# A graph layer over 98 groups of 512 edges: the edge attributes of the next group in five transfers of two tiles, each behind another product of the present group

## The chip, the cores and the metric

The kernel runs on one core of one Trainium2 chip. The metric is device microseconds of one execution; of three runs of the kernel before, the median is 1954.64 us (1952.21 to 1956.52). The profile is of one further execution of the same program, by the hardware profiler.

## The reference

A graph layer over 50,000 nodes of 160 values (64 scalars and 32 vectors of 3) and 50,000 edges of 32 attributes (8 scalars, 8 vectors):

```python
tp = fctp_messages(node_features[col], edge_attr_tensor, W1, W2, W3, W4)
messages = tp @ Wm + bm
agg = jax.ops.segment_sum(messages, row, num_segments=N_NODES)
upd = jnp.concatenate([node_features, agg], axis=-1) @ Wu + bu
# node_features + upd is returned; around it:
x = _layernorm(x + _L0_gnn_ref(...), axis=-1)
```

`fctp_messages` multiplies every node value of an edge's source node with every edge attribute and contracts the products with W1 to W4. Everything is float32.

## The kernel before

The edges are cut into 98 groups of 512 (`GE`), the columns of a tile. For each group the kernel

- gathers the 512 node rows by index with four indirect DMAs of 128 rows, issued by POOL (`gather`, L310, into `xg`). Their landing lets ACT spread the vector part (`spread_x`, L366), and PE transpose it into PSUM (L618, L626);
- holds the edge attributes as ten tiles of 512 columns in `e_sb`, in which the 32 attributes are repeated over the 128 partitions. There are two such buffers, for even and odd groups. SP loads them from DRAM (`load_e`, L213 and L217): 2.62 MB a group, the repetition included;
- multiplies the transposed nodes with the edge tiles on DVE into `prod`: `times_xs` (L490, tiles 0 to 3), three times `times_xv` (L502: tiles 0, 1 and 4, 5; then 0, 1 and 6, 7; then 0, 1 and 8, 9) and `times_y` (L510, tiles 4 to 9). These are six counts of the semaphore `multiplied` (`USES` is 6; `times_y` gives two). L518 adds two products;
- contracts the products on PE (L638, L645), forms the messages (L691, L692), sums the rows of edges with the same target within a pair of tiles (L702 to L705), and copies the sums out on ACT (L420, `summed`);
- adds them to the table `agg` in DRAM with four indirect DMAs of 128 rows that accumulate (`scatter`, L327), issued by POOL. As two rows of the same node must not be added at once, the scatters go in pairs, and a pair waits until the pair before has landed (semaphore `scattered`).

There is no scheduler: each engine runs a program written out by hand, in slots, one for each group. In slot s DVE multiplies group s. POOL issues, in this order, two gathers of group s+2, a pair of scatters of group s-3, the other two gathers, the other pair. PE transposes s+1 and contracts s-1. SP, in `slot`, loads the indices of s+4 and of s+1 (`load_dst`, `load_src`; the second waits until DVE has computed the row indices of group s-3, L527 and L536, which comes right after `times_xs` of slot s; it includes `row_sb`, 256 KB), and then, by `load_e`, the edge attributes of s+2. During slots 0 to 3 SP also writes the start value of `agg` (50 transfers of 640 KB, L236); the first scatter waits for all of them. After the last group a second part of 49 steps reads `agg` and the nodes, adds, normalizes and writes the result (L563 to L588, L447, L347); its node loads (L275) start when PE is done with the groups, its first load of `agg` (L281) when the last scatter has landed.

An engine's instructions wait in the order in which they stand. Semaphores alone tie the engines together.

Of the kernel before, what the change touches and what calls it, by code (L numbers as in the profile page):

```python
# [20 lines left out]
GE = P * TILES  # L21
D = 160
NS, NV, DE = 64, 32, 32
ET = 10
NPROD = 22
USES = 6
# [7 lines left out]
def shift(group, by, m=M1):  # L34

    j, u = group
    return j + (u + by) // m, (u + by) % m


def number(group, m=M1):  # L40
    return group[0] * m + group[1]


def at_least(group, least, m=M1):

    return not isinstance(group[0], int) or number(group, m) >= least
# [14 lines left out]
def build(nc, x, x_rows, x_t, dst_idx, src_idx, src_row, e_rep, w1, w2, w3, w4, wm_t, wu, bu, ident, eye4,  # L61
# [11 lines left out]
    with ExitStack() as ctx:  # L73
# [9 lines left out]
        def sem(name):  # L83
            return ctx.enter_context(nc.semaphore(name))
# [22 lines left out]
        e_sb = two("e_sb", [P, ET, GE])  # L107
# [48 lines left out]
        es_in = [sem(f"es_in{u}") for u in range(M1)]  # L156
        ev_in = [sem(f"ev_in{u}") for u in range(M1)]
# [7 lines left out]
        sp_passed = sem("sp_passed")  # L165
# [23 lines left out]
        multiplied = sem("multiplied")  # L189
# [12 lines left out]
        def hold(engine, passed):  # L202
            engine.sem_inc(passed, 1)
# [2 lines left out]

        @block.sync
        def _(sp):
            def load_e(g):
                if at_least(g, 2):  # L210

                    sp.wait_ge(multiplied, number(g) * USES - 2 * USES + 4)
                sp.dma_start(e_sb[g[1] % 2][:, 0:4, :], e_rep[number(g), :, 0:4, :].unsqueeze(0).to_broadcast([32, 4, 4, GE])  # L213
                             ).then_inc(es_in[g[1]], 16)
                if at_least(g, 2):
                    sp.wait_ge(multiplied, number(g) * USES - 2 * USES + 6)
                sp.dma_start(e_sb[g[1] % 2][:, 4:ET, :], e_rep[number(g), :, 4:ET, :].unsqueeze(0).to_broadcast([32, 4, ET - 4, GE])  # L217
                             ).then_inc(ev_in[g[1]], 16)

            def load_dst(g):  # L220
                if at_least(g, 4):
# [17 lines left out]
            def slot(s):  # L239
                live = lambda d: not isinstance(s[0], int) or 0 <= number(s) + d < n_groups  # L240
                if live(4):
                    load_dst(shift(s, 4))
                if live(1):
                    load_src(shift(s, 1))
                if live(2):
                    load_e(shift(s, 2))
                if isinstance(s[0], int) and number(s) < 4:
                    for k in range(PIECES * (number(s) + 2) // 6, PIECES * (number(s) + 3) // 6):
                        start_table(k)

            for b in range(4):
                load_dst((0, b))
            load_e((0, 0))
            sp.dma_start(start_rows[:, :].rearrange("p (r d) -> p r d", r=SET_ROWS),
                         bu.unsqueeze(0).to_broadcast([P, SET_ROWS, D])).then_inc(start_rows_in, 16)
            for to, frm in (
# [6 lines left out]
            ):  # L263
                sp.dma_start(to, frm).then_inc(consts_in, 16)  # L264
            load_src((0, 0))
            load_e((0, 1))
            sp.wait_ge(start_rows_in, 16)
            for k in range(PIECES * 2 // 6):
                start_table(k)
# [196 lines left out]
        def _(dve):  # L466
# [16 lines left out]

            def times_xs(g):
                dve.wait_ge(A_copied, number(g) + 1)
                dve.wait_ge(es_in[g[1]], g[0] * 16 + 16)
                if at_least(g, 2):

                    dve.wait_ge(rounds, number(g) * ROUNDS - 2 * ROUNDS + 4)
                nc.vector.tensor_tensor(prod[g[1] % 2][:, 0:4, :],  # L490
                                        ps[:, t_bank(g, 0), :].unsqueeze(1).to_broadcast([P, 4, GE]),
                                        e_sb[g[1] % 2][:, 0:4, :], ALU.mult).then_inc(multiplied, 1)

            def times_xv(g, i):
                dve.wait_ge(t_ready, number(g) * USES + 2 + i)
                if i == 0:
                    dve.wait_ge(ev_in[g[1]], g[0] * 16 + 16)
                    if at_least(g, 2):
                        dve.wait_ge(rounds, number(g) * ROUNDS - ROUNDS)
                edge = e_sb[g[1] % 2][:, 0:6 + 2 * i, :] if i == 0 else e_sb[g[1] % 2][:, 0:ET, :]  # L500
# [336 lines left out]
```

## Time and profile before

| | |
|---|---|
| median of three runs | 1954.64 us |
| the profiled execution: its time / its span | 1957.06 us / 1954.9 us |
| PE busy | 1664.8 us (85%) |
| DVE busy | 1548.7 us (79%) |
| POOL busy | 1082.8 us (55%) |
| ACT busy | 894.1 us (46%) |
| bytes moved by DMA | 491.06 MB, mean 251 GB/s |
| share of the 16 DMA engines: SP's queue / POOL's queue | 51.2% / 27.2% |

Busy is the time in which an engine executes an instruction. The issue of a DMA counts as busy on POOL, since POOL writes its own transfers, and doesn't on SP. A DMA's transfer itself is seen in the share of the DMA engines and in the moment at which a waiting instruction is released. In rows of the timeline the bracket at the end is how long the engine was idle before the instruction, and what ended that.

### The profile page before, as it was taken

How to read it: one execution, taken by the hardware profiler on the slowest of the kernel's cores; microseconds unless marked ns; L12 is line 12 of the kernel's file. 1: busy time of each engine (PE TensorE's matmuls, PEld its weight loads, DVE VectorE, ACT ScalarE, POOL GpSimd, SP SyncE). 2: the span in 40 equal slices, each digit the busy share in tenths (PEclk: the TensorE clock that was granted, in tenths of full speed). 3: DMA queues.
4: the chain of work that ended last, by engine and by line, in shares of the span. 5: the costliest groups of instructions: out<-in, count | busy, mean ns of one | idle time of the engine just before them, and what ended most of it. 6: DMA issues, size and time to landing. Idle time of an engine off the chain costs nothing.

```text
span 1954.9 us, 35058 instructions
## 1 busy us (share of the span) xinstructions
PE 1664.8 (85%) x11964; PEld 896.5 (46%) x11964; DVE 1548.7 (79%) x1726; ACT 894.1 (46%) x1721; POOL 1082.8 (55%) x837
## 2 busy tenths in 40 slices
PE   2744999999999999999999999999999999478883
PEld 1312444445444444444444454444444444356662
DVE  2553888888888888888888888888888887089994
ACT  1302444444444444444444444444444444268885
POOL 2104667666666666666666666766666666311110
PEclk9876999999999999999999999999999999889996
DMA  7997777777777777777777777777777875789994
GB/s 246 380 361 234 237 233 224 235 237 231 228 228 226 226 227 226 233 237 236 222 235 240 237 232 229 228 227 225 228 232 238 237 235 121 235 331 420 418 413 178
DMA packets 177240, 491.06 MB, mean 251 GB/s; under 512 B 49560, under 2 KB 101848, under 8 KB 152108
## 3 DMA queue, kind: packets, MB, share of 16 engines
q1 hardware_dynamic: 94892, 381.38, 51.2%
q0 software_dynamic: 82304, 109.12, 27.2%
q8 instruction: 24, 0.39, 0.1%
q14 instruction: 20, 0.16, 0.0%
HBM read 393.52 MB, written 96.88 MB: 251 GB/s over the span
## 4 chain that ended last, share of the span: by engine, by line
DMA 41%; issue 21%; POOL 21%; PE 6%; DVE 5%; SPq 2%; ACT 2%; POOLq 1%; ACTq 0%; DVEq 0%
DMA agg<-summed,row_idx 29%; POOL agg L327 15%; POOL xg L310 6%; DMA prod<-agg 5%; DMA agg<-start_rows 5%; DMA xg<-in_x_rows,dst_sb 3%; DVE stats L582 2%; DVE prod L563 2%; PE ps L638 1%; PE ps L645 1%; SPq L264 1%; DVE mv L588 1%; ACT spread L366 1%; DMA e_sb<-in_e_rep 1%; PE ps L691 1%
## 5 line engine op out<-in xcount | busy, mean ns | idle before, releaser
L327 POOL DMA_INDIRECT agg<-summed,row_idx x392 | 645.0, 1645 | 469.5 <-DMA agg<-summed,row_idx 311.2
L502 DVE TENSOR_TENSOR prod<-ps,e_sb 128x2048 f32<-128x2048 f32 x294 | 663.7, 2285 | 144.1 <-PE ps L645 136.7
L645 PE MATMUL ps<-prod,w_sb 128*32 128x512 f32 x3136 | 753.9, 603 | 0.8 <-ACT S_sb L378 0.8
L310 POOL DMA_INDIRECT xg<-in_x_rows,dst_sb x392 | 411.4, 1050 | 187.8 <-issue 121.8
L366 ACT ACTIVATE spread<-xg 128x1536 f32<-128x1536 f32 x98 | 145.5, 1485 | 435.6 <-DMA xg<-in_x_rows,dst_sb 426.5
L510 DVE TENSOR_TENSOR prod<-ps,e_sb 128x3072 f32<-128x3072 f32 x98 | 328.1, 3348 | 0.0
L490 DVE TENSOR_TENSOR prod<-ps,e_sb 128x2048 f32<-128x2048 f32 x98 | 224.0, 2285 | 111.2 <-ACT A_sb L372 84.1
L645 PEld LDWEIGHTS ps<-prod,w_sb 128*32 128x32 f32 x3136 | 148.6, 109 | 156.4 <-issue 156.4
L638 PE MATMUL ps<-prod,w_sb 128*32 128x512 f32 x1176 | 207.6, 605 | 0.0
L626 PEld LDWEIGHTS ps<-ident_sb,spread 128*128 128x128 f32 x1176 | 127.6, 143 | 170.3 <-issue 121.6
L638 PE MATMUL ps<-prod,sum_sb 128*32 128x512 f32 x1176 | 187.9, 598 | 0.0
L447 ACT ACTIVATE prod<-prod,shift_n,rstd 128x160 f32<-128x160 f32 (+1 forms) x392 | 166.6, 507 | 42.3 <-DVE shift_n L575 42.3
L378 ACT ACTIVATE S_sb<-ps 128x512 f32<-128x512 f32 x98 | 58.8, 600 | 277.4 <-PE ps L645 277.4
L691 PE MATMUL ps<-wc_s,S_sb 128*128 128x160 f32 x784 | 180.8, 311 | 1.2 <-ACT S_sb L378 1.2
L626 PE MATMUL ps<-ident_sb,spread 128*128 128x128 f32 x1176 | 174.0, 285 | 6.7 <-DVE prod L502 4.5
L692 PE MATMUL ps<-wc_v,V_sb 97*128 97x160 f32 x784 | 170.8, 298 | 0.0
L396 ACT ACTIVATE apart<-row_sb,neg_src 128x256 f32<-128x256 int32 x392 | 166.3, 500 | 0.0
L691 PEld LDWEIGHTS ps<-wc_s,S_sb 128*128 128x128 f32 x784 | 124.7, 189 | 83.4 <-issue 81.3
L420 ACT ACTIVATE summed<-ps 128x644 f32<-128x644 f32 x98 | 69.3, 707 | 182.7 <-PE ps L705 135.2
L702 PE MATMUL ps<-msg,same 128*128 128x161 f32 x392 | 100.0, 337 | 45.9 <-ACT msg L412 45.6
L347 POOL DMA_DIRECT2D out<-prod x49 | 26.2, 535 | 203.3 <-ACT prod L447 199.2
L634 PE MATMUL ps<-A_sb,w_sb 64*128 64x512 f32 x392 | 114.4, 661 | 27.3 <-DVE prod L502 27.3
(63 smaller groups left out, 1826.6 us busy)
## 6 DMA issues: line engine op xcount, KB each, us to landing
e_sb<-in_e_rep SPq DMA_DIRECT2D x98, 1536.0 KB
e_sb<-in_e_rep SPq DMA_DIRECT2D x98, 1024.0 KB
agg<-start_rows SPq DMA_DIRECT2D x50, 640.0 KB, 5.4
prod<-agg SPq DMA_DIRECT2D x48, 640.0 KB, 10.4
out<-prod POOLq DMA_DIRECT2D x48, 640.0 KB, 7.7
row_sb<-in_src_row SPq DMA_DIRECT2D x98, 256.0 KB
prod<-in_x_t SPq DMA_DIRECT2D x25, 640.0 KB, 11.9
e_sb<-in_x_t SPq DMA_DIRECT2D x24, 640.0 KB, 12.9
```

The lines of the kernel that those rows point to most:

```text
L310: nc.gpsimd.indirect_dma_start(xg[g[1] % 2][:, q, :], None, x_rows, bass.IndirectOffsetOnAxis(dst_sb[g[1]][:, q:q + 1].bitcast(U32), 0)).t ...
L327: nc.gpsimd.indirect_dma_start(agg, bass.IndirectOffsetOnAxis(row_idx[g[1]][:, q:q + 1].bitcast(U32), 0), summed[g[1]][:, q // 2, q % 2 * ...
L396: last = nc.scalar.activation(apart[:, q, :], pair, ACT.Abs, bias=neg_src[g[1] % 2][:, q:q + 1])
L447: last = nc.scalar.activation(y[0:parts, cols], y[0:parts, cols], ACT.Identity, bias=shift_n[v][0:parts, q:q + 1], scale=rstd[v][0:parts, ...
L490: nc.vector.tensor_tensor(prod[g[1] % 2][:, 0:4, :], ps[:, t_bank(g, 0), :].unsqueeze(1).to_broadcast([P, 4, GE]), e_sb[g[1] % 2][:, 0:4, ...
L502: nc.vector.tensor_tensor(prod[g[1] % 2][:, 4 + 4 * i:8 + 4 * i, :].rearrange("p (a b) e -> p a b e", b=2), ps[:, t_bank(g, 1 + i), :].uns ...
L510: nc.vector.tensor_tensor(prod[g[1] % 2][:, 16:22, :].rearrange("p (f i) e -> p f i e", f=2), ps[:, first:first + 2, :].unsqueeze(2).to_br ...
L626: last = nc.tensor.transpose(ps[:, t_bank(g, 1 + i), q * P:(q + 1) * P], spread[:, q, i * P:(i + 1) * P], ident_sb[:, :])
L638: return nc.tensor.matmul(ps[32 * i:32 * i + 32, V_BANK, :], w, prod[g[1] % 2][:, tile, :], start=start, stop=stop)
L645: return nc.tensor.matmul(ps[32 * quarter:32 * quarter + 32, S_BANK, :], w[:, 32 * half:32 * half + 32], prod[g[1] % 2][:, tile, :], start ...
L691: nc.tensor.matmul(to, S_sb[g[1] % 2][:, q * P:(q + 1) * P], wc_s[:, :], start=True, stop=False)
L692: last = nc.tensor.matmul(to, V_sb[g[1] % 2][:, q * P:(q + 1) * P], wc_v[:, :], start=False, stop=True)
```

## The change

Instead of two transfers (tiles 0 to 3, then 4 to 9) the attributes of a group now come in five of two tiles each, in the order 2, 0, 4, 6, 8. Transfer `step` of group g is issued when `multiplied` has reached (g-1) x 6 + step: the first once all of group g-2 is multiplied, the others one by one behind the products of group g-1. In slot s SP now loads group s+1, not s+2; slot 0 loads none, as groups 0 and 1 are loaded ahead without waits. A small semaphore instruction (`hold`) stands between each wait and its transfer. DVE waits for 32 counts instead of 16 before `times_xs` and for 48 before the first `times_xv`.

```diff
-            def load_e(g):
-                if at_least(g, 2):
-
-                    sp.wait_ge(multiplied, number(g) * USES - 2 * USES + 4)
-                sp.dma_start(e_sb[g[1] % 2][:, 0:4, :], e_rep[number(g), :, 0:4, :].unsqueeze(0).to_broadcast([32, 4, 4, GE])
-                             ).then_inc(es_in[g[1]], 16)
-                if at_least(g, 2):
-                    sp.wait_ge(multiplied, number(g) * USES - 2 * USES + 6)
-                sp.dma_start(e_sb[g[1] % 2][:, 4:ET, :], e_rep[number(g), :, 4:ET, :].unsqueeze(0).to_broadcast([32, 4, ET - 4, GE])
-                             ).then_inc(ev_in[g[1]], 16)
+            def load_tiles(g, t):
+                return sp.dma_start(e_sb[g[1] % 2][:, t:t + 2, :],
+                                    e_rep[number(g), :, t:t + 2, :].unsqueeze(0).to_broadcast([32, 4, 2, GE]))
+
+            def load_e(g, spaced=True):
+
+
+                for step, t in enumerate((2, 0, 4, 6, 8)):
+                    if spaced:
+                        sp.wait_ge(multiplied, (number(g) - 1) * USES + step)
+                        hold(sp, sp_passed)
+                    load_tiles(g, t).then_inc(es_in[g[1]] if t < 4 else ev_in[g[1]], 16)
...
-                if live(2):
-                    load_e(shift(s, 2))
+                if live(1) and at_least(s, 1):
+                    load_e(shift(s, 1))
...
-            load_e((0, 0))
+            load_e((0, 0), spaced=False)
...
-            load_e((0, 1))
+            load_e((0, 1), spaced=False)
...
-                dve.wait_ge(es_in[g[1]], g[0] * 16 + 16)
+                dve.wait_ge(es_in[g[1]], g[0] * 32 + 32)
...
-                    dve.wait_ge(ev_in[g[1]], g[0] * 16 + 16)
+                    dve.wait_ge(ev_in[g[1]], g[0] * 48 + 48)
```

The other engines' instructions stay in their order. On SP, in a slot of the steady part, there stands before (`dst_sb`, `src_sb`, `row_sb` are the indices, `e_sb` the attributes; this is slot 6):

```order
103 L223 DMA dst_sb<-in_dst_idx 128x4 [waits x_gathered2]
104 L230 DMA src_sb<-in_src_idx 128x4 [waits idx_step,apart_done]
105 L231 DMA row_sb<-in_src_row 128x512
106 L213 DMA e_sb<-in_e_rep 128x1x2048 [waits multiplied]
107 L217 DMA e_sb<-in_e_rep 128x1x3072 [waits multiplied]
```

and now (slot 8, the first of the loop's body), where ISA rows are the semaphore instructions and REGISTER_ALU rows compute the loop's waits:

```order
107 L231 REGISTER_ALU [waits idx_step]
108 L232 ISA [waits apart_done]
109 L232 DMA src_sb<-in_src_idx 128x4
110 L233 DMA row_sb<-in_src_row 128x512
111 L218 REGISTER_ALU
112 L210 ISA [waits multiplied]
113 L210 DMA e_sb<-in_e_rep 128x1x1024
114 L218 REGISTER_ALU
115 L210 REGISTER_ALU [waits multiplied]
116 L210 DMA e_sb<-in_e_rep 128x1x1024
117 L218 REGISTER_ALU
118 L210 ISA [waits multiplied]
```

The two transfers of 2048 and 3072 columns have become five of 1024 (the last three stand below the rows shown), each with its own wait.

During the start, SP before issues the attributes of group 2 in slot 0, between the 16th and the 17th transfer of the start value:

```order
40 L230 DMA src_sb<-in_src_idx 128x4
41 L231 DMA row_sb<-in_src_row 128x512
42 L213 DMA e_sb<-in_e_rep 128x1x2048 [waits multiplied]
43 L217 DMA e_sb<-in_e_rep 128x1x3072 [waits multiplied]
44 L236 DMA agg<-start_rows 128x1280 [waits table_set1]
```

and now none there, and those of group 2 a slot (nine transfers of the start value) later:

```order
38 L232 DMA src_sb<-in_src_idx 128x4
39 L233 DMA row_sb<-in_src_row 128x512
40 L238 DMA agg<-start_rows 128x1280 [waits table_set1]
...
48 L238 DMA agg<-start_rows 128x1280 [waits table_set0]
49 L225 DMA dst_sb<-in_dst_idx 128x4 [waits x_gathered1]
50 L232 DMA src_sb<-in_src_idx 128x4
51 L233 DMA row_sb<-in_src_row 128x512
52 L210 DMA e_sb<-in_e_rep 128x1x1024 [waits multiplied] x5
```

Between the first and the last transfer of the start value there stood four groups of attributes (2 to 5), and there stand three now (2 to 4).

## Rows read from the trace of the kernel before

**Rows 1.** Windows view: stretch, its us, busy of the engines, PEclk, DMA share, GB/s.

```profile
300.00:1600.00 1300.00, 1226.76 (x8677) 622.10 (x8676) 1124.67 (x656) 597.05 (x1066) 881.91 (x654) 1.00 0.77 231
```

**Rows 2.** Timeline of DVE: start us, us, instruction, and the idle time before it.

```profile
176.26 2.29 DVE L490 TENSOR_TENSOR prod<-ps,e_sb 128x2048 f32<-128x2048 f32 x1 [39.10 <-ACT A_sb L372]
...
816.02 2.28 DVE L490 TENSOR_TENSOR prod<-ps,e_sb 128x2048 f32<-128x2048 f32 x1
819.83 4.49 DVE L502 TENSOR_TENSOR prod<-ps,e_sb 128x2048 f32<-128x2048 f32 x2 [1.11 <-PE ps L645]
...
827.70 3.35 DVE L510 TENSOR_TENSOR prod<-ps,e_sb 128x3072 f32<-128x3072 f32 x1
832.32 2.29 DVE L490 TENSOR_TENSOR prod<-ps,e_sb 128x2048 f32<-128x2048 f32 x1 [1.27 <-ACT A_sb L372]
...
848.50 2.28 DVE L490 TENSOR_TENSOR prod<-ps,e_sb 128x2048 f32<-128x2048 f32 x1
...
863.32 2.28 DVE L490 TENSOR_TENSOR prod<-ps,e_sb 128x2048 f32<-128x2048 f32 x1
...
1642.49 2.29 DVE L490 TENSOR_TENSOR prod<-ps,e_sb 128x2048 f32<-128x2048 f32 x1 [1.28 <-ACT A_sb L372]
```

**Rows 3.** Waits of PE, 300 to 1600 us: us in total, times, longest.

```profile
PE ps L618 <- DMA xg<-in_x_rows,dst_sb: 34.9, 30, 1.2
```

**Rows 4.** Groups of POOL's instructions, 300 to 1600 us: busy us, mean ns, idle before.

```profile
L327 POOL DMA_INDIRECT agg<-summed,row_idx x328 | 539.9, 1646 | 319.1 <-DMA agg<-summed,row_idx 243.6 <-issue 70.7 <-ACT spread L366 3.7
L310 POOL DMA_INDIRECT xg<-in_x_rows,dst_sb x326 | 342.9, 1052 | 99.3 <-issue 99.3
```

**Rows 5.** Waits of POOL, 300 to 1600 us.

```profile
POOL agg L327 <- DMA agg<-summed,row_idx: 243.6, 91, 4.4
```

**Rows 6.** Timeline of POOL, between 812 and 889 us.

```profile
812.43 1.58 POOL L327 DMA_INDIRECT agg<-summed,row_idx  x1 [0.30 <-ACT spread L366]
...
819.85 1.61 POOL L327 DMA_INDIRECT agg<-summed,row_idx  x1 [3.23 <-DMA agg<-summed,row_idx]
...
882.52 1.61 POOL L327 DMA_INDIRECT agg<-summed,row_idx  x1 [2.19 <-DMA agg<-summed,row_idx]
...
888.94 1.61 POOL L327 DMA_INDIRECT agg<-summed,row_idx  x1 [0.30 <-issue]
```

**Rows 7.** Timeline of SP's queue, the loads issued between 813 and 820 us.

```profile
813.01 0.57 SPq L213 DMA_DIRECT2D e_sb<-in_e_rep  x1
816.27 0.54 SPq L217 DMA_DIRECT2D e_sb<-in_e_rep  x1
...
819.46 0.38 SPq L231 DMA_DIRECT2D row_sb<-in_src_row  x1
```

**Rows 8.** Windows view (columns as in rows 1), four stretches.

```profile
814.00:817.30 3.30, 3.30 (x30) 2.30 (x31) 3.30 (x2) 1.36 (x4) 2.01 (x3) 1.00 0.91 303
...
818.50:822.50 4.00, 4.00 (x30) 1.38 (x25) 2.83 (x3) 2.67 (x6) 2.35 (x2) 1.00 1.01 407
...
826.00:829.00 3.00, 1.82 (x18) 0.71 (x20) 3.00 (x2) 0.72 (x1) 2.39 (x3) 1.00 0.22 40
...
63.00:157.00 94.00, 44.48 (x272) 20.48 (x266) 41.51 (x23) 17.39 (x32) 5.67 (x6) 0.76 0.96 370
```

**Rows 9.** Timeline of POOL: the first scatter, and two of the last.

```profile
162.53 1.62 POOL L327 DMA_INDIRECT agg<-summed,row_idx  x1 [65.95 <-issue]
...
1661.15 1.54 POOL L327 DMA_INDIRECT agg<-summed,row_idx  x1 [2.55 <-DMA agg<-summed,row_idx]
...
1684.27 1.54 POOL L327 DMA_INDIRECT agg<-summed,row_idx  x1 [7.72 <-DMA agg<-summed,row_idx]
```

**Rows 10.** Timeline of SP's queue behind the last group.

```profile
1673.72 4.11 SPq L275 DMA_DIRECT2D prod<-in_x_t  x8
...
1715.98 1.28 SPq L281 DMA_DIRECT2D prod<-agg  x3
```

**Rows 11.** Timeline of DVE behind the last group.

```profile
1681.23 0.22 DVE L527 SCALAR_TENSOR_TENSOR moved<-summed,dup_sb,trash_sb 128x4 f32<-128x4 f32 x1 [9.91 <-ACT summed L420]
```

## The prediction

> **What bounds the kernel now.** I begin with the steady part, 300 to 1600 us, which holds 82 of the 98 groups (82 `times_xs` stand there, a quarter of 328 scatters, [rows 4]). 1300 us / 82 = 15.85 us a group. PE is busy 1226.8 of 1300 us and DVE 1124.7 [rows 1]: PE looks like the bound. The timeline of DVE says otherwise. The starts of `times_xs` lie 16.30, 16.18 and 14.82 us apart [rows 2]. So when nothing is late PE and DVE do a group in 14.82 us, and the mean is 1.03 us above that.
>
> The view of waits names what is late: PE waits for the gathered nodes 30 times in this stretch [rows 3]. Each time two long groups follow each other, as 816.02 to 848.50 does: 32.48 us instead of 2 x 14.82, or 2.84 us lost. 30 x 2.84 = 85 us, which is all of the 1300 - 82 x 14.82 = 85 us above the floor.
>
> Gathers are late because POOL issues them, between scatters. The issue itself takes, per group, 4 x 1.646 + 4 x 1.052 us and eight gaps of 0.30: 6.58 + 4.21 + 2.40 = 13.19 us [rows 4, 6]. That is under 14.82. The rest of 15.85, 2.66 us, is waiting: POOL waits for the landing of scatters 91 times for 243.6 us [rows 5]; without the 0.30 that stand there anyway, 216.3 us, or 2.64 a group and 2.38 a wait. POOL with its landings is the bound, PE stands 1.03 us behind it.
>
> What makes a landing slow? The pair at 882.52 has landed before its successor at 888.94, with only 0.30 idle: 6.42 us a pair [rows 6]. The scatter issued at 812.43 to 814.01 lands so late that the next waits till 819.85, 5.84 us after the issue. In between the first attribute load is in flight (issued 813.01; DMA share 0.91 between 814.0 and 817.3) [rows 7, 8]. Behind the last group, where no attributes are loaded, the wait from issue to landing is 2.55 us; beside the node loads of 640 KB it is 7.72 [rows 9, 10]. And DMA time isn't short as such: the share is 0.77 over the stretch, and 0.22 between 826 and 829 [rows 1, 8]. The attributes come as a block, and a scatter that stands behind the block is held up by it.
>
> **The change, part by part.**
>
> *Size.* At the full rate of 407 GB/s [rows 8] the loads of 4 and 6 tiles take 2.58 and 3.87 us, 6.4 together. A piece of two tiles takes 1.29. If a scatter is held up by the transfer it stands behind, a held-up wait shrinks from 2.38 to 2.38 x 1.29 / 3.22 (the mean of both) = 0.95 us. Bounds: it stays 2.38 (pieces form a train), or it goes to nothing.
>
> The Trainium skill, "DMA: Bandwidth & Descriptors", section "Measured", speaks against the smaller size: batch to at least 1 MiB, and its fit (2.0 us + bytes / 436 GB/s per DMA) would give an estimate of 5 x 3.2 = 16 us a group if the pieces went one after the other. No run shows that here; with several in flight the trace's 640 KB transfers and loads together kept 370 GB/s [rows 8].
>
> *Time of issue.* In a group whose `times_xs` starts at 0, `row_sb` goes out at 3.4 us (819.46 - 816.02) [rows 2, 7]. Now pieces 2 and 0 follow it at once, as their products are done: about 3.9 and 4.5. The others wait for products: piece 4 at 6.1 (the first `times_xv` ends at 819.83 + 2.25), piece 6 at 8.3, piece 8 at 11.7 (`times_y`, the product after it, starts at 827.70). Row and first two pieces make a train of 0.26 + 1.05 MB, 3.2 us; the rest come singly. The slack: piece 8 is needed by the first `times_xv` of the next group, at 14.8 + 3.8 = 18.6, or 6.8 us after its issue; from issue to the end of the first load today it takes 817.3 - 813.0 = 4.3 for twice the bytes. So no new wait on DVE; if the piece were late all the same, each us would be one of the period. SP has three issues of 0.55 us and five semaphore instructions more per slot, while its queue idles most of the slot; indices of s+4 and s+1 stand behind piece 8 and aren't needed for over a slot. Cost nothing, from 0 to 0.2 us a group if that cover were gone.
>
> *Sum of the waits.* Held up as often as now (91 in 82 groups) at 0.95: 1.05 a group, POOL's loop is 14.24 and PE's 14.82 becomes the bound. Held up twice every group at 0.95: 15.09. I expect phases in which it is now one, now the other, and POOL, once ahead, meets the pieces at a fixed place of the slot, where between pieces there is room. I take 14.82 plus one stall in 20 groups (2.84 / 20 = 0.14): 14.96. From `times_xs` of group 5 to that of group 97 it is 1642.49 - 176.26 = 1466.2 us, 15.94 a group [rows 2]; 92 x (15.94 - 14.96) = 90 us saved. Ends: 92 x 1.12 = 103 saved, and 53 lost (the last rival).
>
> *Start.* The first scatter, at 162.53 [rows 9], waits for the start value of `agg`, and the DMA engines are full till then (0.96, 370 GB/s [rows 8]). One group of attributes now comes after instead of before the last transfer of the start value: 2.62 MB / 370 GB/s = 7.1 us earlier. Groups 2 to 4 start later than today, in the shadow of that wait (group 5 stands idle for 39.10 us [rows 2]). Bounds: 0 to 10. Three more issues before the constants cost up to 1.8 us; I take them whole.
>
> *End.* From `times_xs` of the last group to the first load of `agg` it takes 1715.98 - 1642.49 = 73.5 us [rows 2, 10], as POOL comes with a backlog. The last row indices are computed at 1681.23, 38.7 us after `times_xs` [rows 11]. Without backlog two pairs remain from there. Under the node loads a pair costs its issues and the landing, 1.54 + 0.30 + 1.54 + 7.72 = 11.1 us [rows 9]: 38.7 + 22.2 = 61 at best, so 0 to 13 us saved; I take 8, as one more pair may still be in flight.
>
> *Total.* 1957.1 - 90 - 7.1 - 8 + 1.8 = 1853.8 us against the profiled execution's own time (1957.1; its span is 1954.9, with 2.2 us around it, which stay). The median of the runs is 2.4 us below that execution: 1851 us.
>
> **Rivals.**
>
> *One pair stays blocked.* The train of row, pieces 2 and 0 starts right when the row indices release the first pair. It costs that pair what a block costs now, 2.38, the other pair runs free: 13.19 + 2.38 = 15.57, POOL remains the bound. 92 x 0.37 = 34 saved, 7.1 at the start, nothing at the end: 1957.1 - 34 - 7.1 + 1.8 - 2.4 = 1915. For it: a scatter's wait ended only with the whole load at 817.3. Against: under the node loads (the eight of the row in [rows 10] alone are 5.2 MB, 14 us at 370 GB/s, and more follow) a pair took 11.1 us [rows 9], not the length of the queue, so POOL's queue gets its turn within a train.
>
> On that point the skill's page named above, section "Queues, rings and completion order", says that a DMA engine takes turns between queues by packets of several descriptors. By that rule the train is split up and this rival falls; 1915 becomes 1851. It is one reason for my weights.
>
> *Nothing gained.* The same bytes meet the same scatters; the wait per group stays 2.64. Only the start moves: about 1949. For it: bytes are unchanged. Against: the idle share of 0.22 that the spacing would fill.
>
> *Slower.* Now both pairs meet pieces in every group: the first the train at 2.38, the second a single one at 0.95. 3.33 us of waiting instead of 2.66: a period of 13.19 + 3.33 = 16.52. 92 x 0.58 = 53 lost: 1957.1 + 53 - 7.1 + 1.8 - 2.4 = 2002 us. It decides from a mean wait of 15.94 - 13.19 = 2.75 us a group on. For it: the attribute traffic starts at five moments of a slot instead of two, so a pair misses it less often. Against: each hit would have to cost as much as today's.
>
> **How the numbers follow.** Forecast 0.56, one pair blocked 0.26, nothing gained 0.05, slower 0.13. The forecast's own range is 1830 (103, 10 and 13 us saved) to 1885 (two hits a group, 15.09, with little at the ends). To hold 8 in 10 it must reach over the second case: 1832 to 1940. A difference under 0.2% (4 us) can't be told from no change. Faster: 0.56 + 0.26 + 0.02 = 0.84; same 0.03; slower 0.13.
>
> **What would show it.** Right: POOL's waits for the landing of scatters fall under 1.63 us a group (14.82 - 13.19), most with 0.3 to 1 us; the starts of `times_xs` stand 14.82 us apart for long stretches; PE hardly waits for gathered nodes; ACT's copies and DVE don't wait for `e_sb`; the first scatter is issued near 155 us, the first load of `agg` under 70 us after the last `times_xs`. Wrong: the same rhythm of two long groups and a short one (a blocked pair), waits above 2.66 us a group (slower), or DVE waiting for `e_sb`, which would mean that the order and timing of the pieces and not the scatters rule.

## The result: 2008.92 us, slower by 2.9%

| | us, median (range) | ratio to before, 95% interval |
|---|---|---|
| before | 1953.43 (1950.94 to 1956.52) | |
| after | 2008.92 (2003.76 to 2021.68) | 1.0289 [1.0263, 1.0314] |
| forecast | 1851 (1832 to 1940) | |

The time lies outside the range, on the side of the last rival (2002 us). The profiled execution of after took 2021.68 us, 64.6 more than that of before; it is the slowest of the four runs of after (the others took 2003.76 to 2010.78), so the trace shows some 10 us more loss than the medians (55.5 us). First the windows view of after (columns as in rows 1):

```profile
300.00:1600.00 1300.00, 1177.47 (x8260) 593.36 (x8260) 1076.05 (x625) 567.70 (x1014) 816.30 (x625) 1.00 0.80 220
...
826.50:828.40 1.90, 1.90 (x19) 0.66 (x12) 1.90 (x2) 1.47 (x4) 1.28 (x2) 1.00 0.84 77
828.40:834.00 5.60, 4.85 (x36) 2.85 (x38) 5.57 (x4) 0.73 (x1) 1.65 (x2) 1.00 1.01 375
834.00:837.50 3.50, 2.31 (x17) 1.20 (x10) 2.64 (x2) 3.18 (x6) 2.89 (x3) 1.00 0.97 258
```

Beside [rows 1] all five engines are less busy, with the clock as before. The DMA engines are busier (0.80 against 0.77) and move less (220 against 231 GB/s). So a byte takes more of the DMA engines' time than before.

The starts of `times_xs` (now L492) and the first load of `agg`, from the timelines of DVE and of SP's queue (start, us, instruction, idle before it):

```profile
172.15 2.29 DVE L492 TENSOR_TENSOR prod<-ps,e_sb 128x2048 f32<-128x2048 f32 x1 [17.51 <-ACT A_sb L374]
...
820.27 2.29 DVE L492 TENSOR_TENSOR prod<-ps,e_sb 128x2048 f32<-128x2048 f32 x1 [1.75 <-ACT A_sb L374]
...
837.30 2.29 DVE L492 TENSOR_TENSOR prod<-ps,e_sb 128x2048 f32<-128x2048 f32 x1 [0.86 <-ACT A_sb L374]
...
854.22 2.29 DVE L492 TENSOR_TENSOR prod<-ps,e_sb 128x2048 f32<-128x2048 f32 x1 [0.65 <-ACT A_sb L374]
...
1707.18 2.29 DVE L492 TENSOR_TENSOR prod<-ps,e_sb 128x2048 f32<-128x2048 f32 x1
```

```profile
1779.73 1.28 SPq L283 DMA_DIRECT2D prod<-agg  x3
```

From group 5 to 97 it is 1535.0 us against 1466.2 [rows 2]: 16.69 us a group instead of 15.94. These 68.8 us are the whole loss of the profiled run. Group 5 starts 4.1 us earlier, the end takes 72.5 us against 73.5, and 1.3 us more lie behind: 68.8 - 4.1 - 1.0 + 1.3 = 65.0, the difference of the spans. Nearly all groups are now long (17.03 and 16.92 here): 87 of the 92 distances are over 15.2 us, where before it was 73, and 19 were close to 14.82.

Who is late, from the waits and the groups of instructions of after, 300 to 1600 us:

```profile
POOL agg L329 <- DMA agg<-summed,row_idx: 331.4, 129, 4.6
...
PE ps L704 <- ACT msg L414: 79.4, 72, 1.2
...
PE ps L620 <- DMA xg<-in_x_rows,dst_sb: 39.2, 42, 1.8
```

```profile
L329 POOL DMA_INDIRECT agg<-summed,row_idx x313 | 501.4, 1602 | 389.4 <-DMA agg<-summed,row_idx 331.4 <-issue 53.8 <-PE ps L620 2.7
L312 POOL DMA_INDIRECT xg<-in_x_rows,dst_sb x312 | 316.1, 1013 | 95.0 <-issue 95.0
```

A quarter of 313 is 78 groups. POOL waits 129 times (1.65 a group; 1.11 in [rows 5]), and without the 0.30 that stand there anyway 292.7 us: 3.75 a group instead of 2.64, 2.27 a wait instead of 2.38. The issues take 4 x 1.602 + 4 x 1.013 + 2.40 = 12.86, and 12.86 + 3.75 = 16.61 is the period but for 0.08 us. So POOL with its landings still sets it. The wait has kept its size and comes half again as often.

One such wait, in POOL's timeline, in that of SP's queue, and the computing of the row indices in DVE's:

```profile
821.98 1.61 POOL L329 DMA_INDIRECT agg<-summed,row_idx  x1 [0.62 <-issue]
823.90 1.58 POOL L329 DMA_INDIRECT agg<-summed,row_idx  x1 [0.30 <-issue]
...
832.04 1.61 POOL L329 DMA_INDIRECT agg<-summed,row_idx  x1 [3.95 <-DMA agg<-summed,row_idx]
...
839.41 1.61 POOL L329 DMA_INDIRECT agg<-summed,row_idx  x1 [1.26 <-DMA agg<-summed,row_idx]
```

```profile
823.52 0.33 SPq L232 DMA_DIRECT2D src_sb<-in_src_idx  x1
823.96 0.37 SPq L233 DMA_DIRECT2D row_sb<-in_src_row  x1
824.70 9.26 SPq L210 DMA_DIRECT2D e_sb<-in_e_rep  x5
```

```profile
823.04 0.16 DVE L538 TENSOR_TENSOR row_idx<-moved,src_sb 128x4 int32<-128x4 f32 x1 [0.23 <-DVE moved L529]
```

The row indices, ready at 823.20, release SP's index loads, and behind them go pieces 2 and 0; the five pieces start at 824.70, 825.73, 827.78, 829.97 and 833.42. POOL's pair isn't released by these indices: its first scatter starts before them (821.98), as POOL is behind and this pair belongs to an older group. The loads simply start while POOL issues a pair. So it is in 69 of the 78 groups of the stretch: the row indices are ready between the start of a pair's first scatter and the end of its second.

The pair lands 6.56 us after the issue of its second scatter ended (825.48 to 832.04). When that issue ended, only the row and piece 2 were out, 0.79 MB, an estimated 1.9 us at the 407 GB/s of [rows 8]. Without attribute loads a landing took 2.55 us [rows 9], so it takes 4.0 us more here. The DMA view shows what the two queues moved meanwhile (packets, MB, share of the 16 engines; q1 is SP's queue, q0 POOL's). First 825.3 to 828.8 us of after, then 814 to 817 us of before, behind the scatter of 812.43 [rows 6], the second of its pair:

```profile
q1 hardware_dynamic: 168, 0.39, 68.8%
q0 software_dynamic: 1, 0.00, 0.1%
```

```profile
q1 hardware_dynamic: 109, 0.89, 90.6%
```

POOL's queue moves one packet in 3.5 us of after and none in 3 us of before; right behind, it moves 206 packets in 3.2 us and 240 in 2.5 us. In `e3_none` below, without the loads, whose pair is issued from 824.96 to 828.46 us, it moves 140 packets from 827 to 828 us and 144 from 829 to 830. So in both kernels POOL's transfers stand still for about 3 us when a load starts, with 0.89 MB of loads moved in before and 0.39 MB in after. These are two slots and not an average, and whether the scatter's packets were held or not yet there the view doesn't say. But they fit the waits counted above: what holds a pair up hasn't shrunk with the transfer.

### The profile page after: what moved, and what is told of

Its sections match the earlier page's. It is cut to its first block, busy times and chain, and to the rows that moved or that the text cites. A ratio compares the mean times of both kernels' runs of the same rounds, so it can differ in the third digit from the quotient of the medians.

```text
span 2019.9 us, 36588 instructions
## 1 busy us (share of the span) xinstructions
PE 1676.1 (83%) x11964; PEld 897.3 (44%) x11964; DVE 1555.5 (77%) x1726; ACT 894.5 (44%) x1721; POOL 1050.1 (52%) x837
## 4 chain that ended last, share of the span: by engine, by line
DMA 52%; issue 18%; POOL 13%; PE 6%; DVE 5%; SPq 3%; ACT 1%; POOLq 1%; ACTq 0%; DVEq 0%
DMA agg<-summed,row_idx 38%; POOL agg L329 10%; DMA prod<-agg 5%; DMA agg<-start_rows 5%; DMA xg<-in_x_rows,dst_sb 4%; POOL xg L312 3%; DVE stats L584 2%; PE ps L647 1%; DVE prod L565 1%; PE ps L640 1%; SPq L266 1%; SPq L210 1%; DVE mv L590 1%; PE ps L693 1%; ACT same L405 1%
## 5 line engine op out<-in xcount | busy, mean ns | idle before, releaser
L329 POOL DMA_INDIRECT agg<-summed,row_idx x392 | 627.3, 1600 | 554.5 <-DMA agg<-summed,row_idx 431.6
L312 POOL DMA_INDIRECT xg<-in_x_rows,dst_sb x392 | 396.4, 1011 | 199.3 <-issue 121.9
L492 DVE TENSOR_TENSOR prod<-ps,e_sb 128x2048 f32<-128x2048 f32 x98 | 224.3, 2289 | 116.9 <-ACT A_sb L374 71.8
```

Of the source, the lines that this page charges most:

```text
L312: nc.gpsimd.indirect_dma_start(xg[g[1] % 2][:, q, :], None, x_rows, bass.IndirectOffsetOnAxis(dst_sb[g[1]][:, q:q + 1].bitcast(U32), 0)).t ...
L329: nc.gpsimd.indirect_dma_start(agg, bass.IndirectOffsetOnAxis(row_idx[g[1]][:, q:q + 1].bitcast(U32), 0), summed[g[1]][:, q // 2, q % 2 * ...
L492: nc.vector.tensor_tensor(prod[g[1] % 2][:, 0:4, :], ps[:, t_bank(g, 0), :].unsqueeze(1).to_broadcast([P, 4, GE]), e_sb[g[1] % 2][:, 0:4, ...
```

## The experiments

Each ran in three rounds beside the kernel before, whose median was 1953 to 1954 us (1958.67 beside `e5_one`, `e6_row`, `e7_locked` and `e8_block`). The ratios are to these. Ratios stand where the runs of a kernel agree well enough for an interval.

| | attributes of a group | us, median (range) | ratio |
|---|---|---|---|
| `e3_none` | none after group 1 | 1816.55 (1816.11 to 1816.93) | 0.930 [0.9285, 0.9316] |
| before | 4, 6 tiles, old place | 1953.43 | |
| `e1_small` | 5 x 2 tiles, old place | 1973.08 (1968.48 to 1974.27) | 1.0096 [1.0074, 1.0118] |
| `e5_one` | 10 tiles, old place | 1999.27 (1992.35 to 2003.36) | 1.0196 [1.017, 1.0223] |
| `e2_late` | 4, 6 tiles, new place | 2023.66 (2020.25 to 2029.26) | 1.0364 [1.0337, 1.0391] |
| after | 5 x 2 tiles, new place | 2008.92 | 1.0289 [1.0263, 1.0314] |
| `e8_block` | 4, 6 tiles, head of slot | 1999.40 (1993.49 to 2002.88) | 1.0215 [1.0194, 1.0235] |
| `e4_first` | 5 x 2 tiles, head of slot | 1971.63 (1966.33 to 1983.09) | 1.0113 [1.0075, 1.0151] |
| `e7_locked` | 4, 6 tiles, behind landings | 1913.55 (1908.17 to 1921.65) | 0.9784 [0.9759, 0.9809] |
| `e15_locked_small` | 5 x 2 tiles, behind landings | 1987.55 (1980.96 to 1989.9) | 1.0169 [1.0142, 1.0197] |

**Without the loads.** In `e3_none` the slot has no `load_e`:

```diff
-                if live(2):
-                    load_e(shift(s, 2))
...
-                dve.wait_ge(es_in[g[1]], g[0] * 16 + 16)
+                if not at_least(g, 2):
+                    dve.wait_ge(es_in[g[1]], g[0] * 16 + 16)
...
```

DVE's second wait, for `ev_in`, is left out in the same way.

> The kernel before, without the attribute loads of groups 2 to 97 (every later group is multiplied with the attributes of groups 0 and 1, so this part of the input is left out). It prices the loads as a whole. Both theories: POOL's pair falls to about 6.5 us, its loop to 13.2, and PE's 14.82 is the period: 1953 - 92 x 1.1 - about 15 at the start = 1830 to 1850 us. If PE itself is the bound and not POOL's wait for scatters, it stays above 1920.

Its row of the windows view and its waits of POOL, same stretch, and `times_xs` of groups 5 and 97:

```profile
300.00:1600.00 1300.00, 1270.06 (x9111) 660.15 (x9109) 1152.82 (x760) 632.70 (x1133) 913.56 (x669) 0.99 0.44 81
```

```profile
POOL agg L325 <- DVE row_idx L536: 153.4, 83, 5.4
...
POOL agg L325 <- DMA agg<-summed,row_idx: 35.2, 8, 6.9
```

```profile
144.69 2.29 DVE L489 TENSOR_TENSOR prod<-ps,e_sb 128x2048 f32<-128x2048 f32 x1 [38.74 <-PE ps L645]
...
1510.82 2.28 DVE L489 TENSOR_TENSOR prod<-ps,e_sb 128x2048 f32<-128x2048 f32 x1
```

POOL now waits for DVE's row indices: it is ahead. The groups follow each other at 14.85 us. All eight waits for a landing lie behind 1500 us, at the end of the groups; between 300 and 1500 us there is none. Three of them, beside the node loads, are 6.7 to 6.9 us long, the other five, when POOL has no more gathers to issue in between, 2.6 to 4.0. So in the steady part landings hold POOL up only beside attribute loads: this part of the prediction stands. The kernel is 137 us faster. Of these, 1466.2 - 1366.1 = 100 us are the steady part; 31.6 us come from the start, as group 5 starts at 144.69 instead of 176.26. The expectation had 15 us there, and so 1830 to 1850.

**Size alone, at the old place.** `e1_small`, in the kernel before:

```diff
+                for t in (0, 2, 4, 6, 8):
+                    if t == 4 and at_least(g, 2):
+                        sp.wait_ge(multiplied, number(g) * USES - 2 * USES + 6)
+                    sp.dma_start(e_sb[g[1] % 2][:, t:t + 2, :], ...
...
```

DVE waits for 32 and 48 counts, as in after.

> The kernel before with the attributes in five transfers of two tiles, issued at the old times and for the same group (s+2): tiles 0, 2 after four products of group g-2, tiles 4, 6, 8 after its last. Only the size differs from before. Theory P (place): the changed kernel lost its 55 us because its loads now start right behind the row indices, where a pair of scatters is on its way; then size is nearly nothing: 1940 to 1965 us. Theory S (size): many small transfers hold scatters up as much each as a large one, and there are more of them: 1990 to 2020 us. My prediction's step (a hit shrinks with the transfer): clearly under 1953, by 30 us or more.

Measured: 19 us slower, between the two theories and far from my step. POOL's waits:

```profile
POOL agg L326 <- DMA agg<-summed,row_idx: 263.6, 114, 4.4
```

In 81 groups that is 1.41 waits a group, of 2.01 us each above the 0.30.

`e5_one` has one transfer of ten tiles, behind the second wait, so that its first four tiles also come later than before:

```diff
+                    sp.wait_ge(multiplied, number(g) * USES - 2 * USES + 6)
+                sp.dma_start(e_sb[g[1] % 2][:, :, :], e_rep[number(g), :, :, :]...
```

> The kernel before with one transfer of all ten tiles per group, issued when group g-2 is multiplied (the time of the second transfer of before). Fewer starts, longer block. If each start of a load holds up POOL's scatters by nearly as much whatever its size (after: 2.27 us a hold-up at 1.65 hold-ups a group, before: 2.38 at 1.11), one start gives fewer hold-ups: 1900 to 1945 us. If the hold-up goes with the size, as my prediction had it, one pair in each group is held up for up to 5 us: 1970 to 2010.

41 us slower than before beside it (1958.67), as the expectation had it for a hold-up that goes with the size. Its waits, and a pair in POOL's timeline with the load that went out before it:

```profile
POOL agg L322 <- DMA agg<-summed,row_idx: 300.0, 80, 4.6
```

```profile
822.46 1.61 POOL L322 DMA_INDIRECT agg<-summed,row_idx  x1 [0.30 <-issue]
...
832.57 1.61 POOL L322 DMA_INDIRECT agg<-summed,row_idx  x1 [4.00 <-DMA agg<-summed,row_idx]
```

```profile
821.26 0.55 SPq L212 DMA_DIRECT2D e_sb<-in_e_rep  x1
```

One wait a group (80 in 80), and 3.45 us long. So three sizes at about one place give 3.45, 2.38 and 2.01 us a wait, but 1.0, 1.11 and 1.41 waits a group. Together that is 3.45, 2.64 and 2.83 us a group, so at this place the two transfers of before are the best of the three. Shorter transfers shorten a wait a little, not in proportion (2.38 to 2.01, where the forecast has 0.95), and there are more of them.

**Place alone.** `e2_late` is after with two transfers instead of five, `e4_first` is after with `load_e` at the head of SP's slot, `e8_block` is both, with its second transfer behind the first product and not the second:

```diff
 e2_late
-                for step, t in enumerate((2, 0, 4, 6, 8)):
+                for step, t, to in ((0, 0, 4), (2, 4, ET)):
...
 e4_first
+                if live(1) and at_least(s, 1):
+                    load_e(shift(s, 1))
                 if live(4):
                     load_dst(shift(s, 4))
...
```

> The changed kernel's slot and waits, but with two transfers as before: tiles 0 to 3 once group g-2 is done (so behind the row indices), tiles 4 to 9 after the second product of group g-1. Only place differs from before. Theory P: 1990 to 2030 us, as slow as the change. Theory S: 1940 to 1965 us.

> The changed kernel with the attribute loads ahead of the index loads in the slot. The first piece no longer stands behind the wait for the row indices but goes out when group g-2 is done, the second after the first product, so no train of row_sb and two pieces forms; row_sb comes after the fifth piece. Theory P in the form 'the train behind the row indices costs it': back to 1950 or less. Theory S: stays at 2000 to 2020.

> Two transfers (4 and 6 tiles) for group s+1 at the head of slot s: the first when group g-2 is done, the second after the first product of group g-1. It is the kernel with the pieces at the head of the slot (1972 us), with two large ones instead. Theory P: its time is near that one, 1950 to 1990. If small pieces cost 19 us at any place, as they did at the old one: 1945 to 1960.

The waits of POOL in `e2_late`, `e4_first` and `e8_block`, 300 to 1600 us:

```profile
POOL agg L329 <- DMA agg<-summed,row_idx: 310.0, 120, 7.6
```

```profile
POOL agg L329 <- DMA agg<-summed,row_idx: 263.8, 121, 3.7
```

```profile
POOL agg L329 <- DMA agg<-summed,row_idx: 302.9, 79, 5.4
```

The place costs 70 us with two transfers (`e2_late` against before) and 36 with five (after against `e1_small`). Place means here when the loads go out: for group s+1, from the moment of the row indices on, and with five pieces also at five moments instead of two. These parts weren't tried one by one. In after, `load_e` stands behind `load_src`, which waits for the row indices, and the loads then start while POOL issues a pair: in 69 of 78 groups in after, in all 78 in `e2_late`. Taking `load_e` out from behind it gives back 38 us (after to `e4_first`) and 29 (`e2_late` to `e8_block`), each against before beside it.

`e2_late` is what separates place from size. With two large transfers it has 120 waits in 78 groups, 1.54 a group, of 2.28 us each. After has 1.65 of 2.27 us. So at the change's place a wait is as long with transfers of 1.0 and 1.6 MB as with 0.5 MB, and nearly as frequent; against before, it is their number that grew. The medians have the five pieces ahead by 14 us there and by 23 at the head of the slot (`e8_block` to `e4_first`). At the head of the slot the traces show why: two transfers one product apart give one wait a group of 3.53 us, like the single block of `e5_one`, and five pieces apart in time give 1.49 of 1.88 us, 2.81 us a group. At the change's place they don't show the 14 us: the two profiled executions took 2023.65 and 2021.68 us.

`e2_late` came out as theory P had it. `e4_first` (1972) and `e8_block` (1999) met none of the ranges set for them.

**Row behind the pieces.** `e6_row` moves `row_sb` of after behind the fifth piece.

> The changed kernel with the 256 KB of row_sb behind the fifth piece instead of ahead of the first. The place of the pieces stays; only the head of the train is gone. Theory 'the train with row_sb costs it': 1950 to 1975 us. Theory 'the place (behind the row indices) costs it': 2000 to 2015.

Its runs took 1906.07, 1974.7, 1975.25 and 2020.79 us: one program, three different times, at granted clocks of 0.962 to 0.969. It decides nothing on the row, but shows that the kernel can run in more than one way, which the next runs look into. Only the execution of 2020.79 us has a trace.

**Loads that follow the landings.** `e7_locked`, from the kernel before; SP loads group s+1 at the head of slot s, 4 tiles and then 6:

```diff
+                    sp.wait_ge(multiplied, number(g) * USES - USES)
+                if at_least(g, 7):
+                    hold(sp, sp_passed)
+                    sp.wait_ge(scattered, number(g) * 64 - 5 * 64)
+                    hold(sp, sp_passed)
...
+                    sp.wait_ge(multiplied, number(g) * USES - USES + 1)
+                if at_least(g, 7):
+                    hold(sp, sp_passed)
+                    sp.wait_ge(scattered, number(g) * 64 - 5 * 64 + 32)
+                    hold(sp, sp_passed)
...
```

> Two transfers as before (4 and 6 tiles), for group s+1 and at the head of slot s, but each also waits until a pair of scatters has landed: the first for all of group s-5, the second for the first pair of group s-4. So a load goes out just when POOL starts to write the next pair. Theory P (what counts is where a load falls between the scatters): a hold-up gets short, 1870 to 1930 us. If only the number of loads or bytes counts: 1945 to 1975.

Measured: 1913.55 us, as theory P had it. The loads of `e8_block` stand at the same place with the same waits for products, without those for landings, and take 1999.40 us beside it. So with two transfers the waits for landings are worth 86 us.

`e15_locked_small` keeps these waits and issues two and three pieces of two tiles.

> The kernel in which the attribute loads of four and six tiles wait for the landing of a scatter round (1913.6 us), with the same waits and five transfers of two tiles: two behind the first wait, three behind the second. Theory (pieces issued back to back are a train, and hold a scatter as the block does): the same, 1905 to 1930 us, 2.2 us a wait for the landing of scatters, as often as with two. Rival A (smaller transfers let scatters through): waits of under 1.5 us each and 1850 to 1890 us. Rival B (each transfer adds a start of its own): 1930 to 1960 us.

This pair comes nearest to isolating the size, as both waits are the same. The meeting isn't quite: a landing was what released SP's queue 165 times in the 84 groups of `e7_locked`, and 127 times in the 80 of `e15_locked_small`, where the other releases were by products. Waits and DMA queues (packets, MB, share of 16 engines), 300 to 1600 us, of `e7_locked` and then of `e15_locked_small`:

```profile
POOL agg L334 <- DMA agg<-summed,row_idx: 202.7, 91, 5.3
...
q1 hardware_dynamic: 59953, 241.81, 54.3%
```

```profile
POOL agg L338 <- DMA agg<-summed,row_idx: 265.1, 90, 3.9
...
q1 hardware_dynamic: 91516, 229.88, 55.1%
```

About one wait a group in both (91 in 84, 90 in 80), but each takes 2.95 - 0.30 = 2.65 us instead of 1.93, and the kernel is 74 us slower. The loads queue (q1) holds the engines 0.551 x 1300 / 80 = 8.95 us a group instead of 0.543 x 1300 / 84 = 8.40, for the same bytes. The same row for before and for after:

```profile
q1 hardware_dynamic: 58835, 236.73, 48.6%
```

```profile
q1 hardware_dynamic: 89697, 224.74, 52.1%
```

7.70 us a group (82 groups) against 8.68 (78). Part of these 0.98 us comes with the place. Pieces against large transfers at the same place cost 0.47 us a group (`e1_small` 8.17, before 7.70), 0.80 (after 8.68, `e2_late` 7.88) and 0.55 (the pair above). So the pieces are not the same work in smaller portions. But this time in the queue doesn't explain the kernels' times: `e2_late`, at 7.88, is the slowest of all, and `e4_first`, at 9.28 the highest, is faster than after.

My expectation for `e15_locked_small`, that a train of pieces holds a scatter as the block does (1905 to 1930 us), fell; even the rival with a start of its own for each transfer (1930 to 1960) was below the 1987.55 measured. With five pieces the waits for landings gain nothing: `e4_first`, at the same place without them, took 1971.63.

**Backlog.** DVE may begin group 5 only when the scatters of groups 0 and 1 have landed, so POOL enters the steady part without a backlog. The same line in four kernels: after (`e9_after_gate`), before (`e10_before_gate`), `e7_locked` (`e11_locked_gate`) and `e4_first` (`e12_first_gate`); later in `e1_small` (`e13_small_gate`) and `e5_one` (`e14_one_gate`):

```diff
+                if isinstance(s[0], int) and number(s) == 5:
+                    dve.wait_ge(scattered, 16 * TILES * 2)
```

> The changed kernel, with one wait more: DVE begins group 5 only when the scatters of groups 0 and 1 have landed (about 15 us later than now). POOL then enters the steady part without a backlog: its scatter of group g-3 stands about 3 us behind times_xs of group g, where it stands 19 us behind in the changed kernel. Theory B (backlog): the loss is a state in which the loads meet POOL a slot late; without backlog the period is PE's 14.82: 2009 - 92 x 1.85 + 15 = 1840 to 1880 us. Theory P (the place of the loads holds up scatters in any state): the backlog builds up again and the time is 2010 to 2030.

> The kernel before, with the same wait. Theory B: also PE's period, 1860 to 1890 us. Theory P: the backlog builds up again, 1955 to 1970.

> The kernel whose loads also wait for landed pairs (1914 us), with the same wait. Theory B: 1850 to 1880. Theory P: 1915 to 1930, the wait's own cost on top.

> The changed kernel with its attribute loads at the head of the slot (1972 us), with the same wait. Theory B: 1840 to 1880. Theory P: 1975 to 1990.

> The kernel before with its attributes in five transfers of two tiles at the old times, and DVE begins group 5 only when the scatters of groups 0 and 1 have landed, so that POOL starts the steady part without backlog. Theory (the state decides, the size of the pieces hardly): the free state is reached as with two transfers, the starts of times_xs stand 14.8 to 15.0 us apart for long stretches, and the time is 1865 to 1945 us. Rival (more transfers have a price of their own, as in 1973 against 1954 us without the new wait): the backlog comes back within some groups, the period is 16.0 and the time 1970 us.

> The kernel before with one transfer of ten tiles for each group, issued after the sixth product of the group before the last, and DVE begins group 5 only when the scatters of groups 0 and 1 have landed. Theory (a scatter is held up by all that stands before it in the queue, so a block of 2.62 MB costs its whole length once a group if it meets a pair at all): the pair that the block meets waits 3.4 us, the loop of POOL is 13.2 + 3.2 = 16.4 us however it starts, the backlog comes back, and the time is 1980 to 2000 us. Rival (the state decides alone): the block falls between the pairs of a POOL that is ahead, period 14.85, 1865 to 1900 us.

| | us, median (all or range) | ratio |
|---|---|---|
| `e9_after_gate` | 2015.87 (2005.87 to 2030.49) | 1.0300 [1.0272, 1.0328] |
| `e10_before_gate` | 1894.97 (1866.48, 1869.81, 1920.12, 1944.39) | none: far apart |
| `e11_locked_gate` | 1910.30 (1897.62 to 1911.81) | 0.9757 [0.9721, 0.9794] |
| `e12_first_gate` | 1964.36 (1963.32 to 1969.34) | 1.0062 [1.0045, 1.0079] |
| `e13_small_gate` | 1952.53 (1871.68, 1952.38, 1952.69, 1953.14) | none: far apart |
| `e14_one_gate` | 2002.87 (2001.1 to 2005.45) | 1.0257 [1.0239, 1.0275] |

In the profiled execution of `e10_before_gate` (1869.81 us) the period is 14.82 us from end to end. Its waits of POOL (300 to 1600 us, which here takes in some scatters behind the last group), and `times_xs` in DVE's timeline:

```profile
POOL agg L327 <- DMA agg<-summed,row_idx: 181.8, 90, 4.7
```

```profile
812.74 2.28 DVE L490 TENSOR_TENSOR prod<-ps,e_sb 128x2048 f32<-128x2048 f32 x1
...
827.56 2.28 DVE L490 TENSOR_TENSOR prod<-ps,e_sb 128x2048 f32<-128x2048 f32 x1
...
842.43 2.28 DVE L490 TENSOR_TENSOR prod<-ps,e_sb 128x2048 f32<-128x2048 f32 x1
```

(181.8 - 27) / 87 groups = 1.78 us a group instead of 2.64, with the same transfers at the same products. A POOL that is ahead meets the loads at another point. So part of the time of before is its starting backlog, and a run without it can stay without: two of the four runs did. The other two (1920.12 and 1944.39 us) have no trace; that the backlog came back in them on the way is a guess.

After doesn't keep it. The first scatter of the four pairs of `e9_after_gate` behind the gate, and `times_xs` of groups 5, 9 and 11:

```profile
189.16 1.61 POOL L329 DMA_INDIRECT agg<-summed,row_idx  x1 [2.66 <-DVE row_idx L538]
...
200.06 1.61 POOL L329 DMA_INDIRECT agg<-summed,row_idx  x1 [3.83 <-DMA agg<-summed,row_idx]
...
208.90 1.61 POOL L329 DMA_INDIRECT agg<-summed,row_idx  x1 [2.73 <-DMA agg<-summed,row_idx]
...
217.13 1.61 POOL L329 DMA_INDIRECT agg<-summed,row_idx  x1 [2.11 <-DMA agg<-summed,row_idx]
```

```profile
185.73 2.29 DVE L492 TENSOR_TENSOR prod<-ps,e_sb 128x2048 f32<-128x2048 f32 x1 [31.67 <-DMA agg<-summed,row_idx]
...
243.66 2.28 DVE L492 TENSOR_TENSOR prod<-ps,e_sb 128x2048 f32<-128x2048 f32 x1
...
275.99 2.29 DVE L492 TENSOR_TENSOR prod<-ps,e_sb 128x2048 f32<-128x2048 f32 x1
```

The first pair waits for the row indices (POOL is ahead), the next three for landings, 2.1 to 3.8 us each. Up to group 9 the groups take (243.66 - 185.73) / 4 = 14.48 us, the next two 16.2. A POOL that is ahead is held up by the pieces at once, and the backlog is back after five groups. With pieces at the old place (`e13_small_gate`) one run of four took 1871.68 us; in the profiled one (1952.69) the starts lie 14.82 us apart for 26 groups and 16.04 after that. With one block (`e14_one_gate`) the gate gives nothing.

So theory B held for half the runs of before and one of `e1_small`, and for no run of the other four kernels. `e11_locked_gate` and `e12_first_gate`, with 1910 and 1964 us, met neither of their ranges.

## Why the prediction was wrong

**The bound: right.** PE's floor of 14.82 us, and POOL's landings above it, are confirmed by `e3_none` (14.85). The working had small flaws that change nothing in the sum: the loss before isn't 30 regular pairs of long groups, but 63 long groups of 82; 817.3 us is the end of a window and not a landing; and the terms of the 1885 give 1878.

**Price of a hit: the step that failed.** "If a scatter is held up by the transfer it stands behind, a held-up wait shrinks from 2.38 to [...] 0.95 us." It was 2.27 us in after, the same as with two large transfers at that place (2.28, `e2_late`). It was 2.01 in `e1_small`, and with waits for landings it grew (`e15_locked_small`, 2.65 against 1.93). I had the pieces "come singly" behind a train of the row and two. The row and pieces 2 and 0 do go out within 1.8 us of each other, but the others don't stand alone either: from 828.4 to 837.5 us the DMA engines are full (shares of 1.01 and 0.97). And a wait isn't the time of the transfer beside it: POOL's queue stood still for about 3 us in both kernels. The bound "it stays 2.38 (pieces form a train)" stood beside the 0.95, and I chose the other end without a row that showed a wait behind a small transfer. The nearest row was that of the node loads of 640 KB, with 7.72 us [rows 9]. It spoke against me.

**Number of hits: wrong.** I wrote that POOL, once ahead, meets the pieces "where between pieces there is room", and forecast a period of 14.96. It never stays ahead (`e9_after_gate`), the hits are 1.65 a group instead of 1.11, and the wait 3.75 us. `e2_late` has 1.54 hits, so it is the place that brings them. The sum had no term for a load that starts while POOL issues a pair.

The rival "Slower" had this mechanism, more hits, and the sign set for it, over 2.66 us of waiting a group, came true. Its 16.52 us is near the measured 16.69 partly by luck: it had 13.19 + 3.33, measured are 12.86 + 3.75. What its counter-argument asked for, that each hit costs as much as today's, is what happened. It had 0.13.

**Their cost in the queue: missing.** No term of the sum had the 0.5 to 0.8 us a group that the pieces add, at the same place, to the time that loads hold the engines. What it costs the kernel isn't shown: the slowest kernel, `e2_late`, has only 7.88 us of it. The Trainium skill, "DMA: Bandwidth & Descriptors", section "Measured", advises batching to 1 MiB or more for bandwidth. With the waits for landings the runs agree in direction (1913.6 against 1987.6 us), and at the old place (1953.9 against 1973.1); at the head of the slot they don't (1999.4 against 1971.6). The page's fit, which is of transfers that POOL issues, gave an estimate of 16 us a group for transfers one after the other; here they are SP's and several are in flight, and they held the engines for 8.68 us, so no run tests it. And bigger isn't always better: one transfer of 2.62 MB cost 41 us.

**"POOL's queue gets its turn within a train": not borne out as I used it.** By the rule of turns by packets in the Trainium skill, "DMA: Bandwidth & Descriptors", section "Queues, rings and completion order", I weighed the blocked pair down. In the slot shown, POOL's queue moved 1 packet and SP's 168 between 825.3 and 828.8 us, and from there to 832 us 206 and 260. So turns show only in the second stretch, and the pair lands 6.56 us after its last issue instead of the 2.55 us of [rows 9].

**Start: 5.3 us forecast (7.1 less 1.8), within bounds.** The first scatter came 4.3 us earlier (158.23 against 162.53 [rows 9]), group 5 4.1. **End: 8 us forecast, 1.0 measured**; the backlog that was to vanish is there.

**DVE doesn't wait for `e_sb`** in the steady part: right. How much of the slack of 6.8 us was left wasn't measured.

**What stays open.** Why POOL's transfers stand still when loads start, which part of the place (the row indices, group s+1, five moments) brings the hits, and why one program takes 1906 or 2021 us (`e6_row`), 1866 or 1944 (`e10_before_gate`). The two ways of running are shown by the traces of before and `e10_before_gate`; what tips a run from one to the other isn't.

**A faster version.** `e7_locked` and `e11_locked_gate` beat both kernels, by 2.2% and 2.4% over before. `e10_before_gate` has the lowest median of the complete kernels, 1894.97, but not reliably.

## What to carry to other kernels

Where a chain of small dependent DMAs (here accumulating scatters) bounds a kernel, first run it without the bulk loads: that gives the prize (100 us in the steady part here, and 32 at the start). Then move the loads in relation to the chain before cutting them up. With two large transfers, waiting on the chain's own semaphore gave 86 us; with five pieces it gave nothing, so the two have to be tried together. A wait beside a train doesn't shrink with the piece. And ask where a producer's instruction is queued: putting the loads behind another load's wait made them start while a pair was being issued in nearly every group.

## What the runs showed of the hardware that was unexpected

- When a load starts beside a pair of scatters, POOL's queue can stand still for about 3 us, with 0.89 MB of loads moved meanwhile (before, 814 to 817 us) or 0.39 MB (after, 825.3 to 828.8 us).
- In after, the engines are then busy and little moves: a share of 0.84 at 77 GB/s from 826.5 to 828.4 us, all of it packets of SP's queue, then 1.01 at 375. This isn't the start of every train: before moves 303 GB/s at 0.91 between 814.0 and 817.3 [rows 8].
- The same bytes in 512 KB transfers took 6% more queue time a group at the old place (8.17 against 7.70 us) and 10% at the new one (8.68 against 7.88).
- The mean issue of a scatter on POOL isn't constant: 1602 ns in after, 1646 before [rows 4], 1705 in `e7_locked`, 1594 in `e3_none`. Most rows shown have 1.58 or 1.61 us.
